# Neighbour gathers of a two-layer graph network: the neighbour search two tiles ahead of the gathers instead of one

## The chip, the cores and the metric

The kernel runs on one core of a Trainium2 chip. The metric is the device time of one execution in microseconds, the median of several runs. Before the change it is 5430.98 us (three runs, 5403.99 to 5451.06).

## The reference

Two layers over 8 graphs of 2048 nodes with 256 features. Layer 0 takes, for each node, the first 25 neighbours in the 0/1 matrix `adj`, gathers their feature rows, takes the maximum over them, and multiplies node and maximum with a weight matrix. Layer 1 is attention with 4 heads over all neighbours. The cut below leaves out the constants and the second layer's inner part; in the inputs `adj` has only the types 0 and 1.

```
x = _layernorm(x + _L0_gnn_ref(adj, x, L0_gnn_W, L0_gnn_b), axis=-1)
x = _layernorm(x + _L1_gnn_ref(x, adj, ...), axis=-1)

def _L0_gnn_ref(A, X, W, b):
    mask = A != 0
    pri = -jnp.arange(N, dtype=jnp.float32)
    scores = jnp.where(mask, pri, neg_inf)
    vals, idx = jax.lax.top_k(scores, S)            # S = 25
    feats = jax.vmap(lambda x, i: x[i])(X, idx)
    feats = jnp.where(valid[..., None], feats, neg_inf)
    agg = feats.max(axis=2)
    agg = jnp.where((degree <= S)[..., None], jnp.maximum(agg, 0.0), agg)
    h = jnp.concatenate([X, agg], axis=-1)
    return jax.nn.relu(jnp.einsum('bnf,fo->bno', h, W) + b)
```

## The kernel before

The 16384 nodes are 128 tiles of 128 rows; four tiles are a quad, and a graph is 16 tiles. The program is written in steps: step s = 4q + u is step u of quad q. The five engines run the same sequence of steps, each its own share of it (`run_quads`, L90), in straight code for some quads and in loops of one quad for the others. Semaphores alone tie them together. `quad.on(u, lag)` tells whether tile s - lag exists, so a lag of 2 works two tiles behind the step and a lag of -2 two tiles ahead of it.

What happens in step s:

- SyncE loads the rows of `adj` for tile s+2 into `adj_sb` (L383), one buffer that is free once `check` has read it, and the tile's features `xt` (L389), and stores and loads what attention needs.
- ScalarE and TensorE stage the mask of tile s+2: `mask` (L517) makes it 16-bit, `transpose_mask` (L1146) transposes it into `pT`, `check` (L525) reads `adj_sb` again, `transposed` (L542, L546) puts it into `stage` and into the ring `maskT` of six quads, where attention reads it 16 steps later, and `pack_words` (L1160) packs 16 columns to a word in PSUM (`p_key`).
- VectorE searches the words of tile s+1 for the first 25 neighbours: `search_words`, `search_nibbles` and `search_columns`, a chain of 35 dependent links on the semaphore `s_topk`. It ends with the limits `lim` (L762, L763) and the list of row numbers `idx` (L768), each with two buffers, chosen by the tile's parity. Other work is put between the links by number of link (`between`, L980): six masked products of attention, the residual and norm of tile s-1, and at links 12, 19 and 26 the maxima of tile s (CHUNK_AT, L971).
- GpSimd gathers the rows of tile s: 25 indirect DMAs of 128 rows (L498), in five chunks of five, one list column each. Before the tile it waits for the list (`s_idx`, L490), before each chunk for the chunk's buffer in `rows` (`s_rfree`, L494). There is one buffer per chunk; VectorE frees it when it has folded it into `rmax`.
- VectorE folds the chunks: `maximum` (L836) for chunks 0 and 1 together, 2, 3 inside the search, then chunk 4 behind it, then `aggregate` (L845, L846), the maximum over what is left, held within `lim`.
- Behind the gathers follow, in step s and s+1, the transposes of `xt` and `agg` (`transpose_xa`, L1186, and ScalarE's copy L628), `product0`, the norm, `product1` and `project`, all of layer 0 and the projections of layer 1.
- Attention of tile s-16's quad: ScalarE scales (L565), VectorE masks (L819), TensorE multiplies into four PSUM banks (L1231), eight units a step.

Before step 0 ScalarE and TensorE stage the masks of tiles 0 and 1 (L667, L1260) and VectorE searches tile 0 (L1076).

## Time and profile before

| | us |
|---|---|
| median of three runs | 5430.98 (5403.99 to 5451.06) |
| highest of the runs, 2.8 us over the span of the profiled execution | 5451.06 |
| span of the profiled execution | 5448.3 |
| VectorE busy | 4138.1 |
| GpSimd busy | 3717.1 |
| TensorE busy | 3438.2 |
| ScalarE busy | 3111.4 |

An own time of the profiled execution is not listed apart from the three runs; 5451.06 is the nearest to its span. The span runs from the first instruction to the last. A busy time is only how long an engine had an instruction in work. In "idle before" a row tells how long the engine had stood and what released it; "issue" means that the profile shows nothing that it waited for. On GpSimd a gather's time is that of making the DMA, not of moving its rows; the rows' landing shows as a wait of VectorE for "DMA rows".

### The profile page before, as it was taken

Reading aid. Unit: us, or ns where it says so; the run is one execution under the profiler, and the core shown is the slowest. Engines: PE = TensorE matmul, PEld = TensorE weight load, DVE = VectorE, ACT = ScalarE, POOL = GpSimd, SP = SyncE. Lnnn points to the kernel's source line nnn. Section 1 sums busy time; section 2 is a strip of 40 time slices with the busy share of each in tenths; the row PEclk is TensorE's granted clock in tenths of the full one; section 3 lists DMA queues with packets and bytes.
Section 4 is the critical chain, followed back from the end, with each engine's and each line's share of the span. In section 5 each row is a group of like instructions: output and inputs, shape, how many; then the busy total and the mean of one; then the engine's idle time right before and its main releaser. Section 6 shows DMA issues by size and latency. Waiting matters only on the chain.

```text
span 5448.3 us, 58256 instructions
## 1 busy us (share of the span) xinstructions
PE 3438.2 (63%) x11778; PEld 1438.1 (26%) x11778; DVE 4138.1 (76%) x11484; ACT 3111.4 (57%) x5570; POOL 3717.1 (68%) x3204
## 2 busy tenths in 40 slices
PE   1232467666666767666676666666666666666786
PEld 1121222222222222222222222222222222222222
DVE  4555578878787888878787878888878788787777
ACT  3333456666556666656655655656656666555565
POOL 4666777777777777777777777777777777677400
PEclk9555578777778777878777787787888778778798
DMA  3434344444444444444444444444444444444210
GB/s 113 130 119 136 119 138 128 146 132 146 125 129 133 135 144 135 132 143 129 134 133 133 145 125 127 139 130 146 136 144 131 128 139 131 137 131 133 85 39 27
DMA packets 282021, 692.71 MB, mean 127 GB/s; under 512 B 62849, under 2 KB 130178, under 8 KB 265346
## 3 DMA queue, kind: packets, MB, share of 16 engines
q0 software_dynamic: 153600, 419.64, 26.1%
q1 hardware_dynamic: 128130, 270.41, 15.6%
q14 instruction: 257, 2.11, 0.1%
q8 instruction: 34, 0.56, 0.0%
HBM read 639.21 MB, written 50.59 MB: 127 GB/s over the span
## 4 chain that ended last, share of the span: by engine, by line
POOL 36%; issue 25%; DVE 22%; PE 8%; DMA 4%; ACT 3%; another core or an unknown queue 1%; POOLq 0%; DVEq 0%; SPq 0%; ACTq 0%
POOL rows L498 36%; PE acc L1231 5%; DVE uv L819 5%; DVE rmax L836 4%; DMA rows<-in_x_dram,idx 4%; DVE top L715 2%; DVE key_b L717 1%; PE pB L1199 1%; DVE agg L845 1%; DVE sth L892 1%; ACT uv L565 1%; DVE key_a L717 1%; DVE mvh L898 1%; ACT stage L525 0%
## 5 line engine op out<-in xcount | busy, mean ns | idle before, releaser
L498 POOL DMA_INDIRECT rows<-in_x_dram,idx x3200 | 3716.9, 1162 | 1404.5 <-issue 997.0
L1231 PE MATMUL acc<-uv,hs 128*65 128x512 f32 x4096 | 2301.4, 712 | 707.2 <-DVE uv L819 448.3
L565 ACT ACTIVATE uv<-rb,qj 128x512 f32 (+1 forms) x2048 | 1330.4, 712 | 169.6 <-PE acc L1231 137.6
L819 DVE SCALAR_TENSOR_TENSOR uv<-uv,maskT 128x1024 f32<-128x1024 f32 x1024 | 1239.9, 1221 | 183.6 <-ACT uv L565 148.4
L1231 PEld LDWEIGHTS acc<-uv,hs 128*65 128x65 f32 x4096 | 602.6, 160 | 1992.7 <-issue 1403.4
L836 DVE TENSOR_TENSOR rmax<-rmax,rows 128x1280 f32<-128x1280 f32 x384 | 572.5, 1491 | 600.4 <-DMA rows<-in_x_dram,idx 553.5
L628 ACT ACTIVATE xaT<-pA 128x512 f32<-128x512 f32 x128 | 76.4, 597 | 791.3 <-PE pA L1186 610.6
L542 ACT ACTIVATE stage<-pT 128x1024 bf16<-128x1024 f16 x256 | 260.6, 1018 | 288.8 <-remote 148.0
L1186 PE MATMUL pA<-id,xt 128*128 128x128 f32 x256 | 81.5, 419 | 469.4 <-DVE agg L846 334.2
L640 ACT ACTIVATE x1T<-pA 128x256 f32<-128x256 f32 x128 | 49.2, 384 | 570.8 <-PE pA L1209 394.5
L1199 PE MATMUL pB<-w_sb,xaT 128*128 128x256 f32 x1024 | 348.0, 499 | 18.4 <-ACT xaT L628 8.6
L836 DVE TENSOR_TENSOR rmax<-rows 128x1280 f32<-128x1280 f32 x128 | 191.5, 1496 | 172.6 <-DMA rows<-in_x_dram,idx 172.6
L1199 PEld LDWEIGHTS pB<-w_sb,xaT 128*128 128x128 f32 x1024 | 257.0, 262 | 170.6 <-DVE pad L730 87.6
L845 DVE TENSOR_REDUCE agg<-rmax 128x256 f32<-128x1280 f32 x128 | 297.2, 2322 | 4.4
L1209 PE MATMUL pA<-id,xh 128*128 128x128 f32 x256 | 63.2, 334 | 366.1 <-DVE xh L810 341.5
L546 ACT ACTIVATE maskT<-pT 128x1024 f16 (+1 forms) x256 | 260.5, 1018 | 0.0
L1215 PE MATMUL pB<-wcat,x1T 128*128 128x264 f32 x512 | 205.6, 539 | 81.5 <-ACT x1T L640 63.9
L525 ACT ACTIVATE stage<-adj_sb,minus 128x2048 bf16<-128x2048 int32 x128 | 254.1, 1985 | 0.0
L517 ACT ACTIVATE mask_sb<-adj_sb 128x2048 f16<-128x2048 int32 x128 | 243.0, 1898 | 2.0 <-DMA adj_sb<-in_adj_dram 2.0
L715 DVE MAX8 top<-key_a 128x8 f32<-128x104 f32 (+1 forms) x768 | 209.9, 273 | 34.7 <-DVE key_a L717 10.1
L715 DVE MAX8 top<-key_b 128x8 f32<-128x104 f32 (+1 forms) x768 | 207.5, 270 | 35.5 <-remote 20.6
L1160 PE MATMUL pB<-pack,stage 128*128 128x8 bf16 x2048 | 75.3, 169 | 222.6 <-ACT stage L542 221.2
(113 smaller groups left out, 3755.5 us busy)
## 6 DMA issues: line engine op xcount, KB each, us to landing
adj_sb<-in_adj_dram SPq DMA_DIRECT2D x128, 1024.0 KB
rows<-in_x_dram,idx POOLq DMA_INDIRECT x3200
xh_dram<-xh SPq DMA_DIRECT2D x128, 256.0 KB
rb<-r_dram SPq DMA_DIRECT2D x32, 1024.0 KB
xr<-xh_dram SPq DMA_DIRECT2D x64, 512.0 KB
xt<-in_x_dram SPq DMA_DIRECT2D x128, 128.0 KB
out_dram<-xr SPq DMA_DIRECT2D x32, 512.0 KB
r_dram<-er SPq DMA_DIRECT2D x128, 2.0 KB
```

The lines of the kernel that those rows point to most:

```text
L498: nc.gpsimd.indirect_dma_start(rows[:, c, r * C:(r + 1) * C], None, x_rows, bass.IndirectOffsetOnAxis(ap=idx[p][:, k:k + 1], axis=0)).then ...
L517: nc.scalar.activation(mask_sb[:], adj_sb[:], ACT.Sign, accum_out=degree[:, bass.ds(g, 1)]).then_inc(s_mask, 1)
L525: nc.scalar.activation(stage[:].rearrange("p j i -> p (j i)"), adj_sb[:], ACT.Square, scale=2.0, bias=minus1[:], accum_out=adj_sq[:, bass. ...
L542: nc.scalar.activation(stage[:, hf * HALF:(hf + 1) * HALF, :], src, ACT.Square).then_inc(s_stage, 1)
L546: nc.scalar.activation(maskT[:, bass.ds(qg % RING * JT + hf * HALF, HALF), ug * P:(ug + 1) * P], src, ACT.Square).then_inc(s_ring, 1)
L565: last = nc.scalar.activation(uv[k][:, i, :], rb[:, bass.ds(qa % 2, 1), h, :].rearrange("p a i -> p (a i)"), ACT.Copy, scale=q_j(h))
L715: ch.then(nc.vector.max(top[:, k:k + 8], a))
L819: nc.vector.scalar_tensor_tensor(uv[k][:], uv[k][:], 1.0, m, ALU.max, ALU.mult).then_inc(s_u, 1)
L836: nc.vector.tensor_tensor(rmax[:], before, rows[:, c, :], ALU.max).then_inc(s_rfree, 2 if c == 1 else 1)
L845: ch.then(nc.vector.tensor_reduce(agg[:], rmax[:].rearrange("p (r f) -> p f r", f=C), axis=AX.X, op=ALU.max))
L1199: nc.tensor.matmul(p_lin, xaT[:, c, :], w0_sb[:, c, :], start=(c == 0), stop=False)
L1231: last = nc.tensor.matmul(acc[h][0:HW, :], hs[:, (1 - quad.par) * JT + jt, h, :], uv[k][:, i, :], start=(jt == 0), stop=(jt == JT - 1))
```

## The change

The search runs two tiles ahead of the gathers (AHEAD = 2) and the staging of masks three ahead (FRONT = 3), in all engines that take part: SyncE's loads of `adj`, ScalarE's `mask`, `check` and `transposed`, TensorE's `transpose_mask` and `pack_words`. `idx` and `lim` have four buffers, chosen by the step in the quad. Ahead of step 0 three masks are staged instead of two and two tiles are searched instead of one. The old constant AHEAD of attention's scaled units is now called SCALE_AHEAD, with the same value 3.

```diff
@@ constants
+AHEAD = 2
+FRONT = AHEAD + 1
...
-AHEAD = 3
+SCALE_AHEAD = 3
@@ buffers
-        lim = [sb(f"lim{p}", [P, 2], F32) for p in range(2)]
-        idx = [sb(f"idx{p}", [P, S], U32) for p in range(2)]
+        lim = [sb(f"lim{p}", [P, 2], F32) for p in range(QT)]
+        idx = [sb(f"idx{p}", [P, S], U32) for p in range(QT)]
@@ SyncE
-            sp.wait_ge(s_adjread, 1)
-            sp.dma_start(adj_sb[:], adj_rows[P:2 * P, :]).then_inc(s_adj, 16)
+            for g in range(1, FRONT):
+                sp.wait_ge(s_adjread, g)
+                sp.dma_start(adj_sb[:], adj_rows[g * P:(g + 1) * P, :]).then_inc(s_adj, 16)
...
-                if quad.on(u, -2):
+                if quad.on(u, -FRONT):
...
-                    sp.dma_start(adj_sb[:], adj_rows[bass.ds((s + 2) * P, P), :]).then_inc(s_adj, 16)
+                    sp.dma_start(adj_sb[:], adj_rows[bass.ds((s + FRONT) * P, P), :]).then_inc(s_adj, 16)
@@ GpSimd
-                            bass.IndirectOffsetOnAxis(ap=idx[p][:, k:k + 1], axis=0)).then_inc(s_rows[c], 16)
+                            bass.IndirectOffsetOnAxis(ap=idx[u][:, k:k + 1], axis=0)).then_inc(s_rows[c], 16)
@@ ScalarE
-                if quad.on(u, -2):
-                    mask(quad, u, 2)
+                if quad.on(u, -FRONT):
+                    mask(quad, u, FRONT)
...
-            for g in range(2):
+            for g in range(FRONT):
                 mask(Quad(act, 0, 0, 0), 0, g)
@@ VectorE
-                p = (u + g_of) % 2
+                p = (u + g_of) % QT
...
-                nc.vector.tensor_scalar(agg[:], agg[:], lim[u % 2][:, 0:1], lim[u % 2][:, 1:2], ALU.max, ALU.min).then_inc(s_agg, 1)
+                nc.vector.tensor_scalar(agg[:], agg[:], lim[u][:, 0:1], lim[u][:, 1:2], ALU.max, ALU.min).then_inc(s_agg, 1)
...
-                    search_words(quad, u, 1, search)
+                    search_words(quad, u, AHEAD, search)
...
-            search = Chain(dve, s_topk)
-            search_words(Quad(dve, 0, 0, 0), 0, 0, search)
+            for g in range(AHEAD):
+                search = Chain(dve, s_topk)
+                search_words(Quad(dve, 0, 0, 0), 0, g, search)
@@ TensorE
-                for v in quad.reach(lambda q: QT * q + u + g_of - 2):
+                for v in quad.reach(lambda q: QT * q + u + g_of - FRONT):
                     pe.wait_ge(s_proj, v)
...
-                if quad.on(u, -1):
-                    for v in quad.reach(lambda q: QT * q + u + 2):
+                if quad.on(u, -AHEAD):
+                    for v in quad.reach(lambda q: QT * q + u + AHEAD + 1):
                         pe.wait_ge(s_keyread, v)
```

VectorE in its second search of the program, the one of tile 1; before:

```order
L736 TENSOR_SCALAR high<-topi 128x26 [waits s_topk]
L738 TENSOR_SCALAR part<-topi 128x26 x4
L742 TENSOR_TENSOR value<-high,nibkey 128x104 [waits s_topk]
L836 TENSOR_TENSOR rmax<-rows 128x1280 [waits s_rows1,s_rows0]
L744 SCALAR_TENSOR_TENSOR key_b<-part,value 128x104 [waits s_topk]
L745 TENSOR_TENSOR key_a<-part,key_b 128x104 [waits s_topk]
```

And in the changed kernel, whose lines are numbered one higher here:

```order
L737 TENSOR_SCALAR high<-topi 128x26 [waits s_topk]
L739 TENSOR_SCALAR part<-topi 128x26 x4
L743 TENSOR_TENSOR value<-high,nibkey 128x104 [waits s_topk]
L745 SCALAR_TENSOR_TENSOR key_b<-part,value 128x104 [waits s_topk]
L746 TENSOR_TENSOR key_a<-part,key_b 128x104 [waits s_topk]
L716 MAX top<-key_a 128x8 [waits s_topk]
```

The maximum of tile 0's first chunks stood inside the search of tile 1; that search now runs ahead of step 0 with nothing between its links, and the maxima of tile 0 stand in the search of tile 2.

VectorE at the end of step 0, from the limits to the clamp of `agg`; the number behind `lim` and `idx` is the buffer. Before:

```order
L762 TENSOR_SCALAR lim1<-top 128x1 [waits s_topk]
L763 TENSOR_SCALAR lim1<-top 128x1
L765 TENSOR_SCALAR pad<-top 128x25
L766 TENSOR_TENSOR pad<-pad,top 128x25 [waits s_topk]
L767 TENSOR_SCALAR pad<-pad 128x25 [waits s_topk]
L768 TENSOR_SCALAR idx1<-pad,rowbase 128x25 [waits s_topk]
L148 ISA
L836 TENSOR_TENSOR rmax<-rmax,rows 128x1280 [waits s_rows4,s_rfree]
L845 TENSOR_REDUCE agg<-rmax 128x256 [waits s_rfree]
L846 TENSOR_SCALAR agg<-agg,lim0 128x256 [waits s_maxc]
```

After:

```order
L763 TENSOR_SCALAR lim2<-top 128x1 [waits s_topk]
L764 TENSOR_SCALAR lim2<-top 128x1
L766 TENSOR_SCALAR pad<-top 128x25
L767 TENSOR_TENSOR pad<-pad,top 128x25 [waits s_topk]
L768 TENSOR_SCALAR pad<-pad 128x25 [waits s_topk]
L769 TENSOR_SCALAR idx2<-pad,rowbase 128x25 [waits s_topk]
L150 ISA
L837 TENSOR_TENSOR rmax<-rmax,rows 128x1280 [waits s_rows4,s_rfree]
L846 TENSOR_REDUCE agg<-rmax 128x256 [waits s_rfree]
L847 TENSOR_SCALAR agg<-agg,lim0 128x256 [waits s_maxc]
```

Nothing has moved here: in the same places the step writes the list and the limits of tile 2 instead of tile 1, and uses those of tile 0.

GpSimd in its first loop, from the last chunk of a quad's second tile to the first of its third; before:

```order
L498 DMA rows<-in_x_dram,idx1 128x256 [waits s_rfree]
L498 DMA rows<-in_x_dram,idx1 128x256 x4
L490 REGISTER_ALU
L494 ISA [waits s_idx]
L498 DMA rows<-in_x_dram,idx0 128x256 [waits s_rfree]
L498 DMA rows<-in_x_dram,idx0 128x256 x4
```

After:

```order
L499 DMA rows<-in_x_dram,idx1 128x256 [waits s_rfree]
L499 DMA rows<-in_x_dram,idx1 128x256 x4
L491 REGISTER_ALU
L495 ISA [waits s_idx]
L499 DMA rows<-in_x_dram,idx2 128x256 [waits s_rfree]
L499 DMA rows<-in_x_dram,idx2 128x256 x4
```

The third tile of a quad takes its list from a buffer of its own; waits and gathers stand as they did.

## Rows read from the trace of the kernel before

**Rows 1.** The page: span, and busy time, share and instructions of each engine.
```profile
span 5448.3 us, 58256 instructions
...
PE 3438.2 (63%) x11778; PEld 1438.1 (26%) x11778; DVE 4138.1 (76%) x11484; ACT 3111.4 (57%) x5570; POOL 3717.1 (68%) x3204
```

**Rows 2.** The page: chain that ended last, shares by engine and by line.
```profile
POOL 36%; issue 25%; DVE 22%; PE 8%; DMA 4%; ACT 3%; another core or an unknown queue 1%; POOLq 0%; DVEq 0%; SPq 0%; ACTq 0%
POOL rows L498 36%; PE acc L1231 5%; DVE uv L819 5%; DVE rmax L836 4%; DMA rows<-in_x_dram,idx 4%; DVE top L715 2%; DVE key_b L717 1%; PE pB L1199 1%; DVE agg L845 1%; DVE sth L892 1%; ACT uv L565 1%; DVE key_a L717 1%; DVE mvh L898 1%; ACT stage L525 0%
```

**Rows 3.** Waits of the whole span: us in total, times, longest.
```profile
POOL rows L498 <- issue: 997.0, 3116, 1.5
DVE rmax L836 <- DMA rows<-in_x_dram,idx: 726.1, 339, 11.1
ACT xaT L628 <- PE pA L1186: 610.6, 100, 13.5
...
POOL rows L498 <- DVE idx L768: 407.5, 84, 43.0
...
DVE uv L819 <- ACT uv L565: 148.4, 154, 6.5
```

**Rows 4.** Line L498: duration ns min/median/max, first and last start in us.
```profile
L498 POOL DMA_INDIRECT rows<-in_x_dram,idx x3200: 943/950/2254, 43.4 to 5120.9; - x189
```

**Rows 5.** Timeline of GpSimd around tiles 61 and 62 (start, length, idle before).
```profile
2441.06 1.15 POOL L498 DMA_INDIRECT rows<-in_x_dram,idx  x1 [0.30 <-issue]
2443.68 0.94 POOL L498 DMA_INDIRECT rows<-in_x_dram,idx  x1 [1.47 <-issue]
...
2486.01 1.46 POOL L498 DMA_INDIRECT rows<-in_x_dram,idx  x1 [6.41 <-DVE idx L768]
```

**Rows 6.** Timeline of VectorE, same stretch: lists and maxima.
```profile
2442.55 0.24 DVE L768 TENSOR_SCALAR idx<-pad,rowbase 128x25 uint32<-128x25 f32 x1
2450.30 1.49 DVE L836 TENSOR_TENSOR rmax<-rmax,rows 128x1280 f32<-128x1280 f32 x1 [7.51 <-DMA rows<-in_x_dram,idx]
...
2465.47 1.49 DVE L836 TENSOR_TENSOR rmax<-rows 128x1280 f32<-128x1280 f32 x1
...
2484.88 0.24 DVE L768 TENSOR_SCALAR idx<-pad,rowbase 128x25 uint32<-128x25 f32 x1
2485.16 1.49 DVE L836 TENSOR_TENSOR rmax<-rmax,rows 128x1280 f32<-128x1280 f32 x1
```

**Rows 7.** Two stretches: length, busy us (instructions) by engine, PEclk, DMA share, GB/s.
```profile
43.00:650.00 607.00, 178.59 (x856) 113.56 (x854) 311.16 (x1026) 204.80 (x393) 409.10 (x400) 0.61 0.41 126
1000.00:5000.00 4000.00, 2682.33 (x9180) 1107.53 (x9179) 3202.54 (x8934) 2413.54 (x4337) 2954.22 (x2496) 0.79 0.44 135
```

**Rows 8.** Waits of VectorE from 1000 to 5000 us.
```profile
DVE rmax L836 <- DMA rows<-in_x_dram,idx: 508.7, 262, 8.1
...
DVE rmax L836 <- issue: 41.8, 11, 6.9
```

**Rows 9.** Timelines of the start: VectorE, GpSimd.
```profile
30.76 0.29 DVE L728 SCALAR_TENSOR_TENSOR key_b<-pB,wordkey 128x128 f32<-128x128 f32 x1 [8.92 <-PE pB L1160]
...
42.20 0.24 DVE L768 TENSOR_SCALAR idx<-pad,rowbase 128x25 uint32<-128x25 f32 x1
...
76.43 0.95 POOL L498 DMA_INDIRECT rows<-in_x_dram,idx  x1 [0.49 <-issue]
...
122.50 1.41 POOL L498 DMA_INDIRECT rows<-in_x_dram,idx  x1 [13.65 <-DVE idx L768]
```

**Rows 10.** A hold-up, timelines of VectorE and GpSimd.
```profile
3246.23 1.23 DVE L819 SCALAR_TENSOR_TENSOR uv<-uv,maskT 128x1024 f32<-128x1024 f32 x1 [6.51 <-ACT uv L565]
...
3249.75 1.46 POOL L498 DMA_INDIRECT rows<-in_x_dram,idx  x1 [9.52 <-DVE idx L768]
```

**Rows 11.** Lines L836 and L819: duration ns min/median/max.
```profile
L836 DVE TENSOR_TENSOR rmax<-rmax,rows x384: 1472/1493/1549, 64.4 to 5123.8; 128x1280 f32<-128x1280 f32 x192
...
L819 DVE SCALAR_TENSOR_TENSOR uv<-uv,maskT x1024: 1190/1219/1279, 655.0 to 5412.4; 128x1024 f32<-128x1024 f32 x171
```

More of the change, by code:

```diff
@@ L371, in _ @@
             sp.dma_start(adj_sb[:], adj_rows[0:P, :]).then_inc(s_adj, 16)
-            sp.wait_ge(s_adjread, 1)
-            sp.dma_start(adj_sb[:], adj_rows[P:2 * P, :]).then_inc(s_adj, 16)
+            for g in range(1, FRONT):
+                sp.wait_ge(s_adjread, g)
+                sp.dma_start(adj_sb[:], adj_rows[g * P:(g + 1) * P, :]).then_inc(s_adj, 16)
             def step(quad, u):
                 s, p = QT * quad.q + u, u % 2
-                if quad.on(u, -2):
-                    for v in quad.reach(lambda q: QT * q + u + 2):
+                if quad.on(u, -FRONT):
+                    for v in quad.reach(lambda q: QT * q + u + FRONT):
                         sp.wait_ge(s_adjread, v)
                         sp.sem_inc(s_go["sp"], 1)
-                    sp.dma_start(adj_sb[:], adj_rows[bass.ds((s + 2) * P, P), :]).then_inc(s_adj, 16)
+                    sp.dma_start(adj_sb[:], adj_rows[bass.ds((s + FRONT) * P, P), :]).then_inc(s_adj, 16)
                 if quad.on(u, 0):
@@ L587, in step @@
                     last.then_inc(s_sT, 1)
-                scaled_units(quad, u, AHEAD, 4)
-                if quad.on(u, -2):
-                    mask(quad, u, 2)
+                scaled_units(quad, u, SCALE_AHEAD, 4)
+                if quad.on(u, -FRONT):
+                    mask(quad, u, FRONT)
                 if quad.on(u, 1):
@@ L603, in step @@
                     project(quad, u)
-                if quad.on(u, -2):
-                    check(quad, u, 2)
+                if quad.on(u, -FRONT):
+                    check(quad, u, FRONT)
                 scaled_units(quad, u, 6, 7)
-                if quad.on(u, -2):
-                    transposed(quad, u, 2)
+                if quad.on(u, -FRONT):
+                    transposed(quad, u, FRONT)
                 scaled_units(quad, u, 7, 8)
@@ L629, in step @@
                 if next_attends:
-                    for n in range(1, AHEAD):
+                    for n in range(1, SCALE_AHEAD):
                         scaled(quad, u, n, 1)
@@ L977, in step @@
             def step(quad, u):
-                ahead, behind, att, gather, fin = (quad.on(u, lag) for lag in (-1, 1, QT * BQ, 0, FIN))
+                ahead, behind, att, gather, fin = (quad.on(u, lag) for lag in (-AHEAD, 1, QT * BQ, 0, FIN))
                 def between(place):
@@ L998, in step @@
                     search = Chain(dve, s_topk, between)
-                    search_words(quad, u, 1, search)
+                    search_words(quad, u, AHEAD, search)
                     search_nibbles(search)
-                    search_columns(quad, u, 1, search)
+                    search_columns(quad, u, AHEAD, search)
                     assert search.n == LINKS
@@ L1074, in general_tile @@
                 ch.end()
-            search = Chain(dve, s_topk)
-            search_words(Quad(dve, 0, 0, 0), 0, 0, search)
-            search_nibbles(search)
-            search_columns(Quad(dve, 0, 0, 0), 0, 0, search)
+            for g in range(AHEAD):
+                search = Chain(dve, s_topk)
+                search_words(Quad(dve, 0, 0, 0), 0, g, search)
+                search_nibbles(search)
+                search_columns(Quad(dve, 0, 0, 0), 0, g, search)
             run_quads(dve, step)
@@ L1189, in product0 @@
             def product0(quad, u):
-                if quad.on(u, -1):
-                    for v in quad.reach(lambda q: QT * q + u + 2):
+                if quad.on(u, -AHEAD):
+                    for v in quad.reach(lambda q: QT * q + u + AHEAD + 1):
                         pe.wait_ge(s_keyread, v)
@@ L1250, in step @@
                 attend(quad, u, 4, 6)
-                if quad.on(u, -2):
-                    transpose_mask(quad, u, 2)
+                if quad.on(u, -FRONT):
+                    transpose_mask(quad, u, FRONT)
                 attend(quad, u, 6, 7)
-                if quad.on(u, -2):
-                    pack_words(quad, u, 2)
+                if quad.on(u, -FRONT):
+                    pack_words(quad, u, FRONT)
                 if quad.on(u, 0):
@@ L1258, in step @@
                 attend(quad, u, 7, 8)
-            for g in range(2):
+            for g in range(FRONT):
                 transpose_mask(Quad(pe, 0, 0, 0), 0, g)
```

1 line of the change is left out of this document (removed).

## The prediction

> **What bounds the kernel now.** I read the page first: its busy shares, then the chain that ended last, then the waits, then one tile's worth of timeline on GpSimd and VectorE. Busy shares alone name nobody: VectorE is busiest with 76% [rows 1]. But the chain spends 36% of the span in the gathers of L498 and another 25% in "issue" [rows 2], and the waits say what that "issue" is: GpSimd sits 997.0 us before 3116 gathers for nothing that the profile shows, some 0.3 us each, and 407.5 us before 84 gathers for the index list of L768 [rows 3]. The reader should see that GpSimd does nothing but the 3200 gathers, from 43.4 to 5121.9 us: 43.4 us before the first, 3716.9 us in them, 1361.5 us between them (997.0 + 407.5, less the 43.0 of the first wait), and 326.4 us of attention after the last one [rows 1, 3, 4].
>
> One tile shows the loop [rows 5, 6]. The list of tile 62 is written at 2484.88, 0.28 us before the last maximum of tile 61, and the gathers of tile 62 start at 2486.01, after GpSimd has stood for 6.41 us. In that cycle the list of tile s+1 comes only after the third maximum of tile s, because the chunk maxima are placed inside the search; the third maximum needs chunk 3 of tile s; and that chunk needs the list of tile s. So both engines wait for each other: VectorE for rows, 726.1 us in all, GpSimd for lists. Neither is at its limit.
>
> The two limits, from the stretch 1000 to 5000 us [rows 7, 8]. It holds 2496 gathers, 99.8 tiles, so a tile takes 40.06 us. GpSimd: 2954.2 us busy are 29.6 us a tile (1.184 each), and 25 gaps of 0.31 add 7.75: 37.35 us. VectorE waits for rows 508.7 + 41.8 us there, 5.5 us a tile, and everything else that it does or waits for takes 40.06 - 5.5 = 34.5 us. So with the cycle cut GpSimd sets the pace and VectorE has about 3 us of air per tile. Before attention begins, 43 to 650 us, 16 tiles (400 gathers) take 607 us, 37.9 each, against 25.6 us of gathers (1.023 each) and 7.75 of gaps, 33.3 us.
>
> **The change, step by step.** No instruction of the main loops is added, removed or moved against its neighbours: what changes is which tile the search and the mask stages work on. The mask of tile s+3 is staged in step s and searched in step s+1, as before with one less; so the waits among ScalarE, TensorE, SyncE and the search keep their distance. Only the list is now ready one step before its gathers, and the limits of `lim` and the lists have four buffers, since two would be overwritten.
>
> *The list waits go.* If GpSimd never waits, the 3199 gaps are like those inside a tile, 0.30 or 0.31 us [rows 5]. At 0.31 they make 991.7 us of the 1361.5: 369.8 us are saved. Most of that is the wait for lists; the rest stands in gaps of 1.3 to 1.5 us at tile boundaries that the profile calls "issue". I count those as list waits too, since they end at the same distance from their list: for tile 61 the list was done at 2442.55 + 0.24 and the gather came at 2443.68, 0.89 us later; for tile 62 it was done at 2485.12 and the gather came at 2486.01, again 0.89 [rows 5, 6]. Where the list was early, tile 1 in the start, the boundary took 0.49 us [rows 9]. The bounds of this term: 0.30 at each of 127 boundaries, and 1.47.
>
> *What is late next: the rows' buffers.* Chunk c of the next tile may be fetched once chunk c of this one has been folded in. From the last maximum of a tile, at 2450.30, VectorE reaches the next tile's first after 15.2 us and its last after 34.9 [rows 6]. The rows of that last maximum were late themselves: its gather had ended at 2442.21 and it still waited 7.51 us for them to land [rows 5, 6]. So the first chunk buffer comes free up to 8.1 + 15.2 + 1.5 = 25 us after the last gather of the tile before, and GpSimd wants it 37.35 us after that gather: a margin of 12 us, of more where the rows land quickly. The larger hold-ups, such as the 9.52 us of GpSimd after VectorE waited 6.51 us for ScalarE [rows 10], would now be swallowed instead of passed on. I charge nothing; what a hold-up has above 12 us is passed on in full. The mask staged in a quad's second step now opens the next block of the ring `maskT`, a step sooner; its last reader, L819 in the quad before, has run by then, so that wait stays empty.
>
> *Gathers get longer.* The median gather takes 950 ns, the longest 2254 [rows 4]; the mean is 1.023 where VectorE is busy 51% of the time (311.2 of 607) and 1.184 where it is 80% (3202.5 of 4000) [rows 7]. So work of VectorE beside a gather prolongs it. The same 32.1 us of VectorE a tile (3202.5 over 99.8 tiles) will now lie in about 37.8 us, 85%. Above the shortest gather, 0.943, that mean stands by 0.24; in proportion to VectorE's share it grows by 0.24 x 5/80, +0.015 us a gather, and 0.37 a tile; along the line between the two stretches +0.028 and 0.7 a tile. I take 0.45, near the first because the work is the same and only less of it falls beside an idle GpSimd. Over 112 tiles with attention: 50 us given back; bounds 0 and 80.
>
> *Start and end.* Searching tile 1 ahead of the first step takes VectorE some 12 us (the first search ran from 30.76 to 42.44), beside the gathers of tile 0, for whose rows it waits 11.1 us today [rows 3, 9]; the third mask is staged in that time too. So nothing. GpSimd's 13.65 us before tile 2 [rows 9] belong to the 369.8. The 326.4 us behind the last gather hold 16 attention steps and stay.
>
> Sum: a span of 5448.3 - 369.8 + 50 = 5128.5 us. The highest of the three runs, 5451.06, is the span and 2.8 us around it, so the profile stands 20 us over the median of 5430.98. Part of the spread between runs is hold-ups that a GpSimd-bound kernel absorbs, so I carry half of the 20 over: 5128.5 + 2.8 - 10 = 5121, say 5120 us.
>
> **Rivals.**
> 1. *The boundary gap is a fixed cost.* The "issue" gaps of 1.3 to 1.5 us repeat to the hundredth, and the wait for a list is an instruction of its own in front of each tile. For it: the profile itself names nobody there. Against it: 0.49 us at tile 1. Then 127 x 1.16 = 147 us of the saving do not come: 5120 + 147 = 5267 us, or 5190 if half of it stays. Still faster. 16%.
> 2. *VectorE takes over.* The row waits also give ScalarE and TensorE time; in the hold-up of [rows 10] VectorE waited 6.51 us for a scaled unit of L565. If 34.5 us grow past 37.8, the new limit is VectorE; if all 5.5 us come back as waits for L565 and for products, nothing is gained. For it: ScalarE waits 610.6 us for L1186 and VectorE 148.4 for L565 [rows 3], so one chain runs through all three. Against: the step between the last maxima at 2450.30 and 2485.16 had no row wait and took 34.9 us [rows 6]. With 39 us a tile it is 5120 + 112 x 1.2 = 5255, with all 5.5 us back about 5440, no change. 5% and 6%.
> 3. *Gathers and VectorE exclude each other* (ends slower). A tile has eight masked products of 1.22 us and four maxima of 1.49 [rows 11], 15.7 us of long operations with two inputs. If each held GpSimd for its whole length once gathers never pause, a tile would take 23.6 (25 of the shortest gathers, 0.943) + 15.7 + 7.75 = 47.1 us, 7 more than now over 112 tiles: 6230 us. It turns to slower once these operations hold more than 40.06 - 23.6 - 7.75 = 8.7 us a tile. Today the prolongation is 29.6 - 23.6 = 6.0 us with gathers running 37 of 40 us, so it would have to rise by half for 6% more overlap. 4%, and mostly just over the line, about 5500 us.
>
> The Trainium skill (SBUF — State Buffer, "Who interferes with whom") has this rule: a VectorE instruction with two SBUF inputs contends with a GpSimd instruction that reads SBUF, and whoever comes second is blocked until the other is through. The gathers read their list from SBUF. By the rule in full the tile would take the 47.1 us above. The trace agrees in kind, gathers run to 2254 ns beside a median of 950, but not in size, and VectorE's own times do not move: L836 takes 1472 to 1551 ns [rows 4, 11].
>
> **Chances.** Forecast 69%; rival 1 16%; rival 2 5% faster in part and 6% level; rival 3 4%. Faster by over 1% (what a measurement of this kernel can tell from no change): 69 + 16 + 5 = 0.90; within 1%: 0.06; slower: 0.04. The range: below, no stretch and gaps of 0.30 give 5448 - 385 = 5063, with the median's 20 us 5045 to 5065, so 5055; above it must reach into rival 1, half way to its full price: 5235.
>
> **What would show it.** Right: the wait for L769 on GpSimd falls to the first 43 us; gaps at tile boundaries are under 0.6 us, a tile takes 37.5 to 38 us, VectorE still waits some 3 us a tile for rows, and a gather takes about 1.20 us. Rival 1: boundary gaps of 1.3 to 1.5 us in every tile. Rival 2: row waits gone, GpSimd waiting for `s_rfree`, that is for L837, and waits for the scaled units of L566 grown. Rival 3: gathers of 1.3 us and more. A time above 5260 would make the reading of the boundary or of VectorE's air wrong.

## The result, and the profile after

The changed kernel took 5535.1 us (median of 4 runs, 5509.0 to 5544.7) against 5436.2 us for before beside it (4 runs, 5404.0 to 5451.1): 1.0165 of before, 95% interval 1.0111 to 1.0219. The forecast was 5120 us and faster by 6%. The profiled execution has a span of 5507.2 us, 58.9 more than before's.

The same kernel, unaltered, later took 5098.0 us on a chip where before takes 5351.0, a ratio of 0.9536, and 5101.0 us on another (experiments 2). First the profile of the recorded run; I call its chip the recorded chip. Its span, its chain and its gathers, for [rows 1, 2]:

```profile
span 5507.2 us, 58308 instructions
...
DVE 27%; issue 19%; POOL 16%; PE 15%; another core or an unknown queue 12%; ACT 9%; DMA 1%; ACTq 0%; DVEq 0%; POOLq 0%; SPq 0%
...
L499 POOL DMA_INDIRECT rows<-in_x_dram,idx x3200 | 3739.7, 1169 | 1437.6 <-issue 1039.0
```

The gathers have left the chain (36% before, 16% now). "Another core or an unknown queue" has gone from 1% to 12%: time in which an engine waited for a semaphore whose update the profile cannot put down to an instruction. The mean gather, 1169 ns, has hardly grown. The waits, for [rows 3] (us in total, times, longest):

```profile
POOL rows L499 <- issue: 1039.0, 3159, 16.5
...
ACT xaT L629 <- remote: 392.6, 32, 29.0
...
POOL rows L499 <- DVE rmax L837: 355.3, 40, 16.8
...
DVE uv L820 <- ACT uv L566: 245.2, 173, 12.5
...
DVE r L779 <- remote: 189.0, 31, 21.5
DVE key_b L729 <- remote: 165.9, 19, 26.2
...
DVE rmax L837 <- DMA rows<-in_x_dram,idx: 106.7, 46, 6.6
...
POOL rows L499 <- DVE idx L769: 43.4, 1, 43.4
```

Two things that the change was to do, it did: GpSimd waits for a list only once, in the first 43 us, and VectorE's wait for rows fell from 726.1 to 106.7 us. But GpSimd now stands 355 us for free row buffers (L837 increments `s_rfree`). Counted from the gathers themselves, it has 50 gaps of over 0.6 us, 420 us more in sum than gaps of 0.3 would be: 46 stand before a tile's first chunk, and 48 end 0.8 to 1.2 us after the maximum that frees the buffer. From tile 1 on every list was written at least 15 us before its gathers started. And VectorE and ScalarE have new waits, of up to 29 us, that the profile calls "remote". All three are waits for TensorE: L779 for `s_lin`, L729 for `s_key`, L629 for `s_xaT`. One of these hold-ups, in the timeline around tile 84:

```profile
3400.74 1.26 PE L1172 MATMUL acc<-id,sT 65*128 65x65 f32 x16 [2.58 <-issue]
...
3405.34 0.69 PE L1202 MATMUL pB<-b_sb,ones_row 1*128 1x256 f32 x2
3405.55 0.95 POOL L499 DMA_INDIRECT rows<-in_x_dram,idx  x1 [0.31 <-issue]
3406.80 0.95 POOL L499 DMA_INDIRECT rows<-in_x_dram,idx  x1 [0.30 <-issue]
...
3414.93 0.39 DVE L861 RECIPROCAL rden<-acc 128x4 f32<-128x4 f32 x4 [10.50 <-remote]
...
3419.30 0.95 POOL L499 DMA_INDIRECT rows<-in_x_dram,idx  x1 [0.30 <-issue]
...
3423.32 0.42 DVE L779 SCALAR_TENSOR_TENSOR r<-pB,xt 128x256 f32<-128x256 f32 x1 [6.09 <-remote]
...
3427.84 1.65 POOL L499 DMA_INDIRECT rows<-in_x_dram,idx  x1 [7.59 <-DVE rmax L837]
```

TensorE is through with the transposes (L1172) at 3402.0, and VectorE, which waits for just these, goes on at 3414.93. TensorE is through with the product (L1202) at 3406.0, and its reader L779 starts at 3423.32. The results were there; the semaphore updates came 12.8 and 17.3 us late. From 3405.55 to 3420.25 GpSimd issues gathers without a break, each at its shortest, since VectorE stands. Then no buffer is free and GpSimd stops. The first of the two updates came while it was still gathering, the second 3 us after it had stopped.

To count this I set each TensorE update in the trace against the end of the matmul that makes it. Late by over 2 us (and under 25, since a longer distance can be a missing record), and the longest (the expectations of e1, e3 and e5 quote an earlier count with a limit of 40 us, hence 14 and 41 of `s_lin` there):

```
                    s_key        s_xaT        s_lin        s_back      s_T
before               1,  2.4      0           3,  6.9      4,  4.5    59, 13.0
after               37, 21.6     27, 23.6    31, 17.4     11, 13.8    27, 24.4
```

(`s_back` tells that attention's blocks are transposed, `s_T` that half a mask is.)

Updates of VectorE and ScalarE that come once a tile (in before those of L768, L846, L628, L663 and others) are not late in this way. SyncE is slow at times too: some of its register and semaphore instructions take 0.7 us, where 0.02 to 0.06 is usual. And of some 75,700 semaphore updates that the trace should have, before's has 40,596 and after's 32,859.

### The profile page after: what moved, and what is told of

It reads as the page before. It is cut to its first block, busy times and chain, and to the rows that moved or that the text cites. A ratio compares the mean times of both kernels' runs of the same rounds, so it can differ in the third digit from the quotient of the medians.

```text
span 5507.2 us, 58308 instructions
## 1 busy us (share of the span) xinstructions
PE 3399.5 (62%) x11778; PEld 1421.4 (26%) x11778; DVE 4129.9 (75%) x11484; ACT 3106.5 (56%) x5570; POOL 3739.9 (68%) x3204
## 4 chain that ended last, share of the span: by engine, by line
DVE 27%; issue 19%; POOL 16%; PE 15%; another core or an unknown queue 12%; ACT 9%; DMA 1%; ACTq 0%; DVEq 0%; POOLq 0%; SPq 0%
POOL rows L499 16%; PE acc L1233 8%; DVE uv L820 8%; DVE rmax L837 4%; ACT uv L566 4%; DVE top L716 2%; PE pB L1201 2%; DVE agg L846 2%; DVE key_b L718 2%; PE pB L1217 1%; ACT stage L526 1%; ACT maskT L547 1%; DMA rows<-in_x_dram,idx 1%; DVE key_a L718 1%
## 5 line engine op out<-in xcount | busy, mean ns | idle before, releaser
L499 POOL DMA_INDIRECT rows<-in_x_dram,idx x3200 | 3739.7, 1169 | 1437.6 <-issue 1039.0
L1233 PE MATMUL acc<-uv,hs 128*65 128x512 f32 x4096 | 2253.1, 700 | 562.3 <-DVE uv L820 326.7
L566 ACT ACTIVATE uv<-rb,qj 128x512 f32 (+1 forms) x2048 | 1327.4, 711 | 240.0 <-PE acc L1233 143.6
L837 DVE TENSOR_TENSOR rmax<-rmax,rows 128x1280 f32<-128x1280 f32 x384 | 569.2, 1482 | 118.2 <-DMA rows<-in_x_dram,idx 106.0
L1201 PE MATMUL pB<-w_sb,xaT 128*128 128x256 f32 x1024 | 369.0, 523 | 294.0 <-DVE pad L731 153.7
L629 ACT ACTIVATE xaT<-pA 128x512 f32<-128x512 f32 x128 | 76.4, 597 | 728.8 <-remote 392.6
L596 ACT ACTIVATE sd<-mv,eps 128x1 f32<-128x1 f32 x128 | 37.7, 295 | 515.7 <-DVE tick L792 433.6
L846 DVE TENSOR_REDUCE agg<-rmax 128x256 f32<-128x1280 f32 x128 | 299.2, 2337 | 7.4 <-remote 1.6
L779 DVE SCALAR_TENSOR_TENSOR r<-pB,xt 128x256 f32<-128x256 f32 x128 | 53.3, 416 | 272.8 <-remote 189.0
```

What stands on the lines that cost most here:

```text
L499: nc.gpsimd.indirect_dma_start(rows[:, c, r * C:(r + 1) * C], None, x_rows, bass.IndirectOffsetOnAxis(ap=idx[u][:, k:k + 1], axis=0)).then ...
L566: last = nc.scalar.activation(uv[k][:, i, :], rb[:, bass.ds(qa % 2, 1), h, :].rearrange("p a i -> p (a i)"), ACT.Copy, scale=q_j(h))
L837: nc.vector.tensor_tensor(rmax[:], before, rows[:, c, :], ALU.max).then_inc(s_rfree, 2 if c == 1 else 1)
L846: ch.then(nc.vector.tensor_reduce(agg[:], rmax[:].rearrange("p (r f) -> p f r", f=C), axis=AX.X, op=ALU.max))
L1201: nc.tensor.matmul(p_lin, xaT[:, c, :], w0_sb[:, c, :], start=(c == 0), stop=False)
L1233: last = nc.tensor.matmul(acc[h][0:HW, :], hs[:, (1 - quad.par) * JT + jt, h, :], uv[k][:, i, :], start=(jt == 0), stop=(jt == JT - 1))
```

## The experiments

### 1. Pauses and a hold, and the suspected cost by itself

Theory A was that an unbroken train of gathers holds TensorE's updates back; B, that SyncE's loads do it when they meet the gathers; C, that the longer distances cost in themselves; D, that VectorE's own work is the limit.

```
e1: before the gathers of tile s
-  for v in quad.reach(lambda q: QT * q + u + 1):
+  for v in quad.reach(lambda q: TILES if ... else QT * q + u + 2):
       pool.wait_ge(s_idx, v)
e2 (only for c == CH - 1), e3 (every chunk): after the five gathers of chunk c
+  for v in quad.reach(lambda q: 16 * CR * (QT * q + u + 1)):
+      pool.wait_ge(s_rows[c], v)
```

> After, but GpSimd does not start the gathers of tile s before the index list of tile s+1 is out too, so that they start where they started before the change; search, masks and the four index lists stay as the change has them. Theory A (an unbroken train of gathers, or a train that starts early and runs through VectorE's waits, holds TensorE's semaphore updates back): the pause of some 3 us at each tile boundary comes back and drains them, waits for s_key, s_lin and s_back over 2 us get as rare as before (before: 1 of s_key over 2 us, after: 38), time 1.00 of before, 5400 to 5470 us. Theory B (SyncE's big loads meet the gathers): the loads are as in before again in relation to the gathers, so this cannot tell A from B; 1.00 too. Theory C (the longer distance of masks and search by itself, with its other order on VectorE, ScalarE and TensorE): 1.0165 as after, 5500 us or more.

> After, with one more wait on GpSimd: at the end of each tile's 25 gathers it waits until the last five have landed, then goes on to the next tile. The pause should be 1.3 to 2 us (a landing takes some 1.5 us after the gather's end), so 1.0 to 1.7 us per tile more than the 0.31 between gathers. Theory A (trains without a pause hold TensorE's updates back): updates late by over 2 us get rare, VectorE's waits for s_key and s_lin shrink from 189 + 166 us to under 60, undisturbed tiles take 38.5 + 1.3 = 39.8 us: 5330 to 5450 us, ratio 0.98 to 1.00. Theory B (only the meeting of SyncE's loads with the gathers matters): late updates stay, the pause comes on top: 5560 to 5700 us, ratio over 1.02. Theory D (VectorE's own 39.5 us a tile is the bound now, no lag of updates): the pause on GpSimd hides in its waits for s_rfree, ratio 1.015 as after.

> After, with GpSimd waiting for the landing of its five gathers after every chunk: five pauses of 1.3 to 2 us in a tile. Theory A: no TensorE update is late by over 2 us any more; the train grows to 37.2 + 5 x 1.3 = 43.7 us and more, which then is the bound: 44 to 46 us a tile, 5750 to 6100 us, but with waits of GpSimd for s_rfree and VectorE's for s_key and s_lin near zero. Theory B and C: the same train, but the late updates stay as in after (some 38 of s_key, 41 of s_lin over 2 us). The time tells little here, the lags do.

> A kernel of its own: the whole computation is left out (its output is x's first tile only), and it measures the disputed thing alone. Eight stages of 60 rounds each of a ping-pong by semaphore: TensorE does one matmul, VectorE adds and lets TensorE go on; then the same with ScalarE in TensorE's place. Beside each: nothing; 80 gathers of 128 rows back to back on GpSimd; the gathers and 12 loads of 1 MB on SyncE; the loads alone. Theory A: TensorE's rounds get far longer beside the gathers (single updates late by 5 to 20 us), ScalarE's rounds do not. Theory B: only the stage with gathers and loads together shows late updates. Theory C: all stages within 20% of the first, for TensorE and for ScalarE, and the late updates of after come from something else.

Measured, on a chip where before takes 5337.6 us: e1 1.0053 (1.0032 to 1.0073), e2 1.0466 (1.0440 to 1.0492), e3 1.2817 (1.2788 to 1.2847). In none of the three is one TensorE update late by over 2 us, and 75,700 to 75,900 update records are there. In e4 TensorE's round takes 1.739 us and ScalarE's 0.908 in every stage, beside gathers or not, to the hundredth.

So the pauses did not show what I built them for: on this chip there was nothing to cure, and before ran 2% faster too. What they do show is the price of a pause. GpSimd's wait for its own landings does not take the 1.3 to 2 us that I expected:

```profile
POOL rows L499 <- issue: 1035.0, 3099, 6.5
...
POOL rows L499 <- DMA rows<-in_x_dram,idx: 483.0, 98, 9.9
```

That is e2: 4.9 us in each of 98 tiles, so a tile takes 41.5 us. My 1.5 us was the distance between a gather's end and the end of its last DMA packet when nothing else is in flight (1.4 to 1.5 us in e3). At the end of a tile in e2 that packet ends 3.4 us after the gather on average (1.4 to 8.6), and the next gather starts another 1.5 us later. In e3, which I expected at 5750 to 6100 us and which took 6847, the wait is 3.3 us each time (2002.4 us in 610 waits). e1 says that with the gathers held back the rest of the change is worth nothing, 0.5% slower: whatever the change brings or costs, it does by starting the gathers earlier. Theory C is out for a chip like this one.

### 2. Both kernels unaltered, on other chips

> The changed kernel once more, unaltered, since the runs with waits added (on this chip before takes 5338 us, not 5436) showed not one TensorE update late by over 2 us, of any semaphore, where the profiles of before and after both had them (s_T 60 and 30 times, s_key 1 and 38, s_lin 14 and 41). Theory A (the unbroken train holds TensorE's updates back): here too s_key and s_lin are late dozens of times, VectorE waits over 300 us for them, and the time is 1.01 to 1.02 of before. Theory E (the late updates belong to the chip or the loading of the program, and the change only fell on them harder): here none are late, and the change brings what it leaves when they are gone: about 38.3 to 38.7 us a tile against 40.0, ratio 0.96 to 0.98. Theory C (the longer distances cost in themselves): ratio 1.01 or more without any late update.

> The kernel before once more, unaltered, for its profile on this chip. Theory A: as the first profile, some 60 updates of s_T late by over 2 us. Theory E: none late, and a steady tile near 39.2 us where the first profile has 40.0. Either way GpSimd's wait for the list stands at about 3.1 us a tile.

> The changed kernel unaltered on whichever chip this call gets; the first measurement gave 1.0165 with late TensorE updates in both profiles (before 5436 us), the second 0.9536 with none (before 5351 us). Theory E (the late updates belong to a chip or its moment, not to the change): the ratio goes with the time of before: where before takes 5330 to 5360 us the ratio is 0.95 to 0.96 and no s_lin or s_back update is late by 2 us; where before takes 5400 us or more the ratio is 1.00 to 1.02 and some 40 of s_lin are. Theory A alone would give 1.01 to 1.02 on every chip, which the second measurement has already against it.

Measured: after 5098.0 us where before takes 5351.0, ratio 0.9536 (0.9521 to 0.9552); on a further chip 5101.0 against 5344.1, 0.9544 (0.9516 to 0.9571). e6, the same kernel as before, 1.0014 (0.9994 to 1.0034). Theory A as it stood, valid for every chip, would have 1.01 or more; theory E (the place) was right in kind. The gain was larger than it had forecast for e5 (0.96 to 0.98, and 38.3 to 38.7 us a tile, where 37.4 were measured), and before's steady tile did not fall to 39.2 but to 39.7; for e7 it had 0.95 to 0.96. The group of the gathers on the page of e6, before on this chip (count | busy, mean ns | idle before, releaser of most):

```profile
L498 POOL DMA_INDIRECT rows<-in_x_dram,idx x3200 | 3686.5, 1152 | 1337.3 <-issue 939.3
```

The same group on the page of e5, after on this chip:

```profile
L499 POOL DMA_INDIRECT rows<-in_x_dram,idx x3200 | 3745.4, 1170 | 1018.0 <-issue 974.5
```

And all that GpSimd waits for in e5 (us in total, times, longest):

```profile
POOL rows L499 <- issue: 974.5, 3199, 0.3
POOL rows L499 <- DVE idx L769: 43.5, 1, 43.5
```

Here GpSimd's loss is the whole account. Idle time falls from 1337.3 to 1018.0, by 319.3 us, and its 3199 gaps are all 0.3 us; gathers take 58.9 us more. That is 260.4 us, and the span fell from 5350.0 to 5088.7, by 261.3. The chain that ended last, in e5, names one engine:

```profile
POOL 63%; issue 19%; DVE 8%; PE 5%; DMA 2%; ACT 1%; POOLq 1%; SPq 0%; DVEq 0%; ACTq 0%
```

No "remote" wait is left in either of them, and no TensorE update is late by over 0.5 us. From here on I call a chip disturbed where updates come late. A steady tile (mean of tiles 20 to 126, us), as my count of the trace gives it; the step and the two columns of waits are VectorE's, from last maximum to last maximum, the other two GpSimd's:

```
                          step   25 gathers  gap to next  row wait  VectorE's other idle
e6  before, undisturbed   39.70    36.58        3.14        5.80          1.88
e5  after,  undisturbed   37.37    37.09        0.30        3.65          1.84
    before, recorded      40.01    36.89        3.12        5.52          2.41
    after,  recorded      40.23    37.20        3.16        0.74          7.56
```

Read the last two rows against the first two. Undisturbed, the change takes 2.2 us of row wait out of the tile and puts nothing in its place. The recorded after loses 4.8 us of row wait, and pays 5.15 us in other waits of VectorE.

### 3. More updates

Half of the update records were missing on the first chip. If a path of updates is full there, more of them should bring it about elsewhere.

```
  end of SyncE's step
+ sp.wait_ge(s_tiny, 16 * NUPD)
+ sp.sem_clear(s_tiny)
+ for k in range(NUPD):          # NUPD = 48
+     sp.dma_start(tiny_in[:, k * 4:(k + 1) * 4], c_tiny[0:16, 0:4]).then_inc(s_tiny, 16)
  ...  (left out: 48 such loads ahead of the first step, a wait behind the last)
```

> After, with SyncE also starting 48 loads of 256 bytes at the end of each of its steps, where it otherwise waits some 29 us a tile for s_adjread: 768 more semaphore updates by DMAs a tile beside the some 590 that there are, and hardly any bytes. Theory F (the late TensorE and SyncE updates of the first profiles are a path of updates, or of their records, that is full: in those profiles half of the update records are missing, 32859 and 40596 of 75700): with 2.3 times the updates late ones appear here too, s_lin and s_key over 2 us dozens of times, records go missing, ratio 1.00 or more. Theory E (the place, not the load on it): none late, all records there, ratio 0.954 to 0.965.

> The kernel before with the same 48 small loads a tile. Theory F: late TensorE updates appear, fewer than in after with them, ratio 1.01 to 1.03. Theory E: none, ratio 1.00 to 1.01.

> After with 48 small loads a tile more on SyncE (as e8, which gave 1.04 where before takes 5460 us). On an undisturbed chip, theory F (any chip's path of updates fills with 2.3 times as many): dozens of late ones, ratio 1.00 or more. Theory E: none late, all records there, 0.954 to 0.965. On a disturbed one: 1.03 to 1.05 again.

> The 48 small loads a tile once more, for a chip that is not disturbed. Theory F: 2.3 times the updates make late ones there too, ratio 1.00 or more. Theory E: none late, all update records there (some 174000), ratio 0.954 to 0.965. If the chip is a disturbed one: 1.03 to 1.06 as in e8 and e12.

Measured: e8 and e9 fell on a disturbed chip, where before takes 5459.6 us: 1.0406 (1.0255 to 1.0556) for after with the loads. Before with them took 5560 and 5649 us, two runs too far apart for an interval. e12 fell on another, before 5441.6: 1.0527 (1.0437 to 1.0616), where plain after has 1.0215. e15 on an undisturbed one, before 5346.7: 5124.4 us, 0.958, a single run. Of some 174,700 update records 168,136 are there, no wait is for "remote", and GpSimd's gaps are 0.3 us.

So on a disturbed chip the loads make the changed kernel 3% slower (5726.8 against 5550.4 us on the chip of e12), and an undisturbed one carries 2.3 times as many updates at some 0.5%. Theory F is half right: the load matters, but only where the chip is of that kind.

### 4. The same questions on a disturbed chip

e10 is after, unaltered; e11 is the kernel of e1, e13 that of e4.

> The changed kernel unaltered, beside the next three on one chip. So far: where before takes 5338 to 5351 us the ratio is 0.954 and no updates are late; where it takes 5436 us the ratio was 1.0165; and on a chip where it takes 5460 us the extra small loads gave 1.04. Theory E (place): if before takes 5400 us or more here, the ratio is 1.00 to 1.02, with dozens of s_lin and s_key updates over 2 us late and a third or more of the update records missing; if it takes 5360 us or less, 0.95 to 0.96 and none.

> After with the gathers held back to where they started before (as in e1). On an undisturbed chip 1.005 again. On a disturbed one, theory G (there the earlier start of the gathers is what brings the late updates of s_key, s_lin and s_back): they fall back to about the number of before, ratio 0.995 to 1.010, under that of after by 0.7 to 1.5%. Theory H (there masks three ahead and the rest of the change bring them): ratio as after, 1.01 to 1.02, with as many late ones.

> The kernel of e4 again (the whole computation left out), which on an undisturbed chip showed TensorE's rounds never late by more than 1.4 us. On a disturbed one, theory I (gathers alone, back to back, are enough there): TensorE's rounds beside gathers late by 5 us and more, ScalarE's not, SyncE's instructions 0.7 us. Theory J (it takes the whole load of the kernel, the many updates of all engines and SyncE's loads together): all stages as in e4.

Measured beside before at 5441.6 us: e10 1.0215 (1.0136 to 1.0294), e11 1.0114 (1.0041 to 1.0186). The counts of updates late by over 2 us:

```
                    s_key        s_xaT        s_lin        s_back      s_T
e10 after           40, 21.8     33, 18.3    34, 15.6      8, 16.0    32, 22.3
e11 gathers held     0, 1.2       0           6,  8.9      6,  4.4    55, 13.0
```

e11 has the pattern of the recorded before back, with search and masks at the new distance: `s_key` and `s_xaT` are on time, `s_lin` and `s_back` late seldom and for less long, `s_T` often. From the waits of e11:

```profile
POOL rows L499 <- DVE idx L769: 459.2, 79, 55.2
...
DVE r L779 <- remote: 33.4, 7, 11.3
```

And from those of e10, where the same line waits five times as long:

```profile
POOL rows L499 <- DVE rmax L837: 386.6, 47, 21.8
ACT xaT L629 <- remote: 380.7, 39, 26.7
...
DVE key_b L729 <- remote: 184.6, 25, 26.9
...
DVE r L779 <- remote: 171.7, 37, 18.7
```

Theory G holds for the late updates: it is the earlier start of the gathers that brings them, not the rest of the change. For the time it holds too: the intervals of the two ratios overlap, since both contain the spread of before, but the four runs of e11 (5490.0 to 5525.3 us) all lie under the four of e10 (5532.8 to 5584.3). e11's 1.0114 is a little above the 1.010 that I had allowed.

e13 is the clearest run of the study. Eight stages of 60 rounds (one run each of e4 and e13); us per round:

```
                  nothing   gathers   gathers + loads   loads
TensorE, e4        1.739     1.739        1.739         1.739
TensorE, e13       1.740     2.663        2.409         1.740
ScalarE, e4, e13   0.908     0.908        0.908         0.908
```

Gathers alone do it, and to TensorE's rounds, not to ScalarE's: theory I. The timeline of VectorE in e13, whose gathers run from 109 to 208.9 us:

```profile
139.09 0.42 DVE L148 TENSOR_TENSOR d<-pL,xt 128x256 f32<-128x256 f32 x1 [1.32 <-PE pL L172]
143.65 0.42 DVE L148 TENSOR_TENSOR d<-pL,xt 128x256 f32<-128x256 f32 x1 [4.14 <-remote]
149.25 0.42 DVE L148 TENSOR_TENSOR d<-pL,xt 128x256 f32<-128x256 f32 x1 [5.18 <-remote]
154.85 0.42 DVE L148 TENSOR_TENSOR d<-pL,xt 128x256 f32<-128x256 f32 x1 [5.18 <-remote]
...
210.88 0.42 DVE L148 TENSOR_TENSOR d<-pL,xt 128x256 f32<-128x256 f32 x1 [5.17 <-remote]
215.78 0.42 DVE L148 TENSOR_TENSOR d<-pL,xt 128x256 f32<-128x256 f32 x1 [4.48 <-remote]
219.28 0.42 DVE L148 TENSOR_TENSOR d<-pL,xt 128x256 f32<-128x256 f32 x1 [3.07 <-remote]
221.38 0.42 DVE L148 TENSOR_TENSOR d<-pL,xt 128x256 f32<-128x256 f32 x1 [1.68 <-PE pL L172]
223.12 0.42 DVE L148 TENSOR_TENSOR d<-pL,xt 128x256 f32<-128x256 f32 x1 [1.31 <-PE pL L172]
```

For 30 us (24 gathers) nothing happens, then each of TensorE's updates takes 3.9 us longer (5.18 instead of 1.31), always the same, and after the last gather this shrinks to nothing within 14 us. That is how a queue behaves which the gathers fill faster than it drains and through which TensorE's updates pass. That it is a queue is my reading; the rows show the three phases. It would explain why the boundary mattered: a train that stops every 25 gathers and waits 3 us lets it drain in part. It does not explain the size: here an update is 3.9 us late, in the full kernel up to 24 us. It also narrows B: loads of SyncE alone delay nothing here, nor do they lengthen a TensorE round beside the gathers. (Of the rounds with both, 12 take over 2 us, with gathers alone 16; the longest has 5.6 us in either.)

### 5. Gates

If TensorE's updates come through once GpSimd stops (the update at 3414.93 above did not wait for that), GpSimd can be made to stop where one is due, at no cost where it has come already.

```
  before the gathers of chunk c
+ if c == 2:
+     wait for s_key >= s + FRONT (TILES at the end), and for s_xaT >= s
+ if c == (4 if u == 0 else 3):
+     wait for s_lin >= s
```

> After, with three gates for GpSimd in a tile's train of gathers: before the third group of five it waits for TensorE's s_key and s_xaT of the tile that VectorE works on, before the fourth (the fifth in a quad's first tile) for its s_lin. By the profile of e5 these have come by then (s_key by 10.4 us of the train at most, s_xaT by 14.6 with the group at 14.1, s_lin by 23.6 with the groups at 21.8 and 29.8), so on an undisturbed chip the gates cost next to nothing: 0.953 to 0.962 where before takes 5340 to 5360 us. On a disturbed one, theory K (an update of TensorE comes through when GpSimd stops gathering): each late one is let through at the next gate, VectorE's waits for s_key, s_xaT and s_lin get shorter than 10 us, ratio 0.97 to 1.00, under the 1.0165 to 1.0215 of after. Theory L (the gates do not let it through, or only shift the wait to GpSimd): 1.02 or more.

> The kernel of e14 unaltered, for a chip on which TensorE's updates come late (before takes 5430 to 5460 us there; e14 fell on an undisturbed one). Theory K (an update of TensorE comes through when GpSimd stops gathering): ratio 0.97 to 1.00. Theory L (the gates only shift the wait to GpSimd): 1.015 or more. On an undisturbed chip again 0.953 to 0.962.

> The kernel of e14 and e16 once more, for the same question. Where before takes 5430 us or more: theory K (an update of TensorE comes through when GpSimd stops gathering) 0.97 to 1.00; theory L (the gates only shift the wait to GpSimd) 1.015 or more. Where it takes 5360 us or less: 0.953 to 0.962.

> The same kernel a last time, for a chip with late updates. Where before takes 5430 us or more: theory K 0.97 to 1.00, theory L 1.015 or more. Where it takes 5360 us or less: 0.953 to 0.962.

All four fell on undisturbed chips (before 5346.7, 5345.6, 5335.9 and 5352.2 us): 0.9549, 0.9560, 0.9580 and 0.9555, each within 0.3% either way. That is some 10 us over after's 5098 and 5101, and the profile of e14 shows why it is no more: 64 short waits, 27.8 us in sum.

```profile
POOL rows L507 <- PE pB L1210: 14.6, 48, 0.3
POOL rows L507 <- PE pA L1196: 13.2, 16, 3.0
```

Whether they help on a disturbed chip was never measured. The remedy is untested; only its price is known.

## Why the prediction was wrong

*What bounds the kernel.* Right. The cycle from list to gathers to the third maximum to the next list was there, and cutting it made GpSimd the pace: 63% of the chain in e5.

*The list waits go*, 369.8 us. Right in kind and sized on a disturbed profile. The gaps fell to 0.30 on the recorded chip wherever GpSimd was not blocked, so rival 1, the fixed cost of a boundary, is refuted. Against the gaps of e5, the recorded before has 386.5 us of such waits (1404.5 - 1018.0) and the undisturbed one 319.3; the difference stands in the first 16 tiles, whose gaps sum to 82.1 us in the recorded profile and to 13.6 in e6. The 13.65 us before tile 2 [rows 9], which I read as a list wait, was 0.50 us in e6.

*Gathers get longer*, 50 us. Right: 58.9 us, 1152 to 1170 ns, and 0.51 us a tile for the 0.45 I took. Rival 3 (1.3 us and more) is out.

*Start and end*, nothing. Right: the first gather starts at 43.9 us instead of 43.7 in e5 and e6, and 324.8 us follow the last instead of 325.8.

The same sum on the undisturbed profile: 1294.0 us between the gathers of e6, less 991.7, are 302.3 saved, and 5350.0 - 302.3 + 50 = 5097.7 us; the span was 5088.7. The prediction as written, 0.943 of the median, was 1% too good there, for the 67 us of disturbance that it counted as gain. Two bounds of the range do not follow from their words: gaps of 0.30 us everywhere would save 402 us and not 385 (that is 0.305 a gap, which e5 then had), and half way into rival 1 is 5194 us, not 5235. Neither matters for a time of 5535.

*What is late next: the rows' buffers.* This is the step that failed. I gave it a margin of 12 us, charged nothing, and wrote that hold-ups "would now be swallowed instead of passed on". That took the hold-ups of before as fixed in size and number. On the recorded chip they are not: they are late TensorE updates, and the later start of each tile's gathers, with its pause of 3 us at the boundary, kept them short and most of them away, as e10 and e11 show on a chip of this kind. Without it they grew from at most 7 us (but for `s_T`) to 14 to 24 us, past the margin, and GpSimd then waited 355 us for `s_rfree`. The balance by GpSimd's own rows: idle 1437.6 us where it had 1404.5 (997.0 + 407.5), gathers +22.8. Undisturbed, the margin held: not one of e5's gaps is longer than 0.3 us.

*Rival 2*, VectorE takes over, had all the marks that I gave it (row waits gone, waits for `s_rfree`, longer waits for L566) and the wrong engine. VectorE's own work did not grow; its waits for TensorE did. (Its 5440 us is also more than its own terms give: 5.5 us back in each of 112 tiles is 5120 + 112 x 2.2 = 5366, unless the first 16 tiles lose their gain too.) I had bounded it at no change, on the thought that no more than the 5.5 us of row waits could come back. What came back was of another origin, and nothing limited it to 5.5.

Could it have been seen? In part. The waits of before named it, and the prediction did not use this row:

```profile
ACT stage L542 <- remote: 148.0, 37, 9.9
```

In e6, undisturbed, no line of the kernel has a wait for "remote". I took up the hold-up of [rows 10], 6.51 us for a scaled unit, but never asked what had held that unit. It was the same thing. ScalarE works in the order of its program, and just before it had stood for the transposes of L1209, which TensorE had ended at 3232.24:

```profile
3237.05 0.38 ACT L640 ACTIVATE x1T<-pA 128x256 f32<-128x256 f32 x1 [4.42 <-remote]
...
3244.78 1.32 ACT L565 ACTIVATE uv<-rb,qj 128x512 f32 x2
```

That it would grow threefold could not be read from any row.

What stays open. First, what makes a chip disturbed, and whether it is the chip or the moment: it was so for the recorded chip and for two of the eight that the experiments fell on (of which the recorded one may be one), and the only one of the eight that was measured at two times, by e7 and by e16, was undisturbed both times. Second, whether the recording takes part. In every run with late updates 46% or more of the update records were missing, so it may be the writing of records that is backed up, and an execution without a recording might not show it; no run here separates the two. Missing records alone delay nothing: e15 lacks 6,500 of them, and where ScalarE had its rounds beside gathers in e13, 13 of its 60 updates have no record, at 0.908 us a round. In e13 the first of them is missing 8 us after the first gather, and the first late update comes 32 us after it. The Trainium skill (NOTIFIC — Programmer's Manual, "2.4 When the ring fills") has three answers to a full ring of records: by default the new record is lost, a second way overwrites the oldest, and the third makes the producer stall. By what it says of the default, records would be missing and nothing late; the traces of this case show both at once, and no run here tells which setting they had. Third, whether the gates cure it.

## What to carry to other kernels

A wait that you take away may be the pause in which something else drains; before charging nothing for the hold-ups that remain, ask what ended each of them, and look for "remote" among the waits. Check that the profile you size terms on is a clean one: here it had 67 us too many in the very term that the forecast rested on. And where one kernel gives 1.017 and 1.022 in two measurements and, with its gated form counted in, 0.954 to 0.958 on five chips, the chip (or its moment) is a variable of the experiment: measure on several before you keep or drop a change.

## What the runs showed of the hardware

- On a disturbed chip gathers issued back to back delay TensorE's semaphore updates: in a small kernel by 3.9 us, once some 30 us of gathers have gone out (e13), in this one by up to 24 us (after, e10). ScalarE's rounds beside the same gathers stayed at 0.908 us.
- On an undisturbed chip 3200 gathers back to back, with 0.3 us between them, delay no recorded update of TensorE by over 0.5 us (e5), and with 2.3 times the updates there is no wait for "remote" either (e15, one run).
- GpSimd's wait until the last five gathers of a tile have landed takes 4.9 us (e2), and 3.3 us where it waits after every five (e3); the last DMA packet ends 1.4 to 8.6 us after the gather in e2.
- Three more waits in a tile, for semaphores that have mostly been reached, cost GpSimd little between gathers: 64 stops with 27.8 us in sum (e14), and 5108 to 5112 us where the kernel without them took 5098 and 5101.
